# Causal attention with a mixture of experts: the order of value product and output projection within a step

## What is computed

```
x + attention(xn) + ffn(xn)

attention: q = (xn @ Wq + bq).reshape(b, h, t, dh)      16 heads of 128
           k, v = xn @ Wk + bk, xn @ Wv + bv            by head
           softmax(q k^T / sqrt(128), causal) @ v, heads joined, @ Wo + bo
ffn:       a shared expert, plus the best 6 of 64 experts per token,
           each expert with room for 128 tokens
```

## Time and profile before

| | |
|---|---|
| median of 3 runs (lowest, highest) | 2060.81 us (2058.49, 2063.56) |
| the profiled execution, its time | 2065.55 us |
| the profiled execution, its span | 2063.8 us |
| TensorE busy (matmuls) | 1683.7 us, 82% |
| VectorE busy | 1502.6 us, 73% |
| ScalarE busy | 1090.3 us, 53% |
| GpSimd busy | 1101.2 us, 53% |
| granted TensorE clock, mean over the span | 0.925 |

### The profile page before, as it was taken

The page is one execution under the profiler, slowest core; times in us unless marked ns, Lnnn a source line. Parts: engine busy times, 40 slices in busy tenths (PEclk is TensorE's granted clock), DMA queues, the critical chain, the costliest instruction groups (busy, mean ns, idle before and its releaser), DMA issues. The chain is left out here.

```text
span 2063.8 us, 49196 instructions
## 1 busy us (share of the span) xinstructions
PE 1683.7 (82%) x19016; PEld 1307.4 (63%) x19016; DVE 1502.6 (73%) x3148; ACT 1090.3 (53%) x2300; POOL 1101.2 (53%) x920
## 2 busy tenths in 40 slices
PE   1253089999999999999967788899899999888887
PEld 1242067777777777777756666677666666666665
DVE  5598956666667676666634478888888888888875
ACT  1520056666666666666622265555555555555564
POOL 0510046666666666666620066666666666666543
PEclk9676589999999999999977599999999999999999
DMA  5225067777665666656657566667666676667655
GB/s 182 102 102 196 0 129 135 134 136 129 123 110 104 123 103 101 105 103 104 109 130 218 171 112 121 119 120 147 120 122 121 117 139 120 122 119 144 118 90 109
DMA packets 695996, 253.35 MB, mean 123 GB/s; under 512 B 642384, under 2 KB 682145, under 8 KB 695008
## 3 DMA queue, kind: packets, MB, share of 16 engines
q1 hardware_dynamic: 668096, 204.12, 52.7%
q0 software_dynamic: 19232, 37.84, 7.2%
q10 hardware_dynamic: 8448, 8.39, 1.2%
HBM read 61.30 MB, written 54.66 MB: 56 GB/s over the span
## 5 line engine op out<-in xcount | busy, mean ns | idle before, releaser
L448 POOL TENSOR_TENSOR prob<-prob 128x128 f16<-128x128 f32 (+7 forms) x512 | 673.5, 1316 | 809.0 <-ACT prob L784 805.7
L777 ACT ACTIVATE prob<-prob,nmax 128x128 f32<-128x128 f32 (+7 forms) x512 | 398.0, 777 | 625.4 <-DVE prob L1135 568.0
L601 PE MATMUL ps_s<-kT,qT 128*128 128x512 f16 (+3 forms) x2304 | 460.6, 328 | 9.2 <-DVE prob L1135 5.7
L616 PE MATMUL ps_o<-probT,vh 128*128 128x256 f16 (+1 forms) x3840 | 434.4, 267 | 4.9 <-DMA probT<-prob 4.9
L1135 DVE TENSOR_SCALAR_CACHE_REDUCE prob<-ps_s,neg_scale 128x128 f32<-128x128 f32 (+7 forms) x512 | 408.8, 808 | 2.0 <-PE ps_s L603 1.8
L616 PEld LDWEIGHTS ps_o<-probT,vh 128*128 128x128 f16 x3840 | 372.0, 100 | 52.7 <-issue 5.8
L784 ACT CAST prob<-prob 128x128 f16<-128x128 f32 (+7 forms) x512 | 341.3, 667 | 2.9 <-DMA probT<-prob 0.6
L627 PE MATMUL ps_y<-wo,oT 128*128 128x256 f16 x1536 | 212.3, 275 | 126.5 <-DVE oT L1150 115.8
L601 PEld LDWEIGHTS ps_s<-kT,qT 128*128 128x128 f16 x2304 | 201.7, 99 | 162.9 <-issue 19.6
L567 PE MATMUL ps_t<-xT,wq 128*128 128x64 f16 x6144 | 195.2, 194 | 62.4 <-DMA xT<-xn_columns 61.0
L627 PEld LDWEIGHTS ps_y<-wo,oT 128*128 128x128 f16 x1536 | 136.2, 98 | 165.3 <-DVE oT L1150 136.7
(11 more groups left out here) (182 smaller groups left out, 1713.5 us busy)
## 6 DMA issues: line engine op xcount, KB each, us to landing
dispatched<-zeros SPq DMA_DIRECT2D x16, 512.0 KB, 5.4
probT<-prob SPq DMA_TRANSPOSE x512
ex<-dispatched SPq DMA_DIRECT2D x16, 512.0 KB, 4.3
expert_out<-eo ACTq DMA_DIRECT2D x16, 512.0 KB, 3.8
resid<-in_L_attn_x_dram SPq DMA_DIRECT2D x2, 2048.0 KB, 11.2
xn_rows<-xn SPq DMA_DIRECT2D x8, 512.0 KB, 3.0
xn_columns<-xnth SPq DMA_DIRECT2D x16, 256.0 KB, 2.3
xT<-xn_columns SPq DMA_DIRECT2D x8, 512.0 KB, 5.8
```

Of the source, the lines that this page charges most:

```text
L448: pool.tensor_tensor(low_cols(j), prob_cols(j).rearrange("p (r k) -> p r k", k=P), high_cols(j), ALU.subtract).then_inc(p_low, 1)
L601: pe.matmul(s_cols(j, lo, hi), qT[:, u, a, j * P:(j + 1) * P], kT[:, u, c, lo:hi], start=(n == 0), stop=(n == 2 and hi < w))
L616: mm = pe.matmul(ps_o[:, lo:2 * P], vh[:, u, a, r * D:(r + 1) * D], probT[:, PT_AT[c] + 2 * r + s, lo:], start=(r + n == 0), stop=(r == 2 ...
L777: nc.scalar.activation(prob_cols(j), prob_cols(j), ACT.Exp, bias=nmax[:, j:j + 1], scale=-1.0, accum_out=rsum[:, i % 2, j:j + 1]).then_inc ...
```

## The change

Three hand-written orders change; no instruction is added, removed or altered.

```diff
 TensorE, attention()
                     scores(i, 0)
+                    scores(i, 1)
                     if old:
+                        values(i - 1, 1)
                         project_y(i - 1, 0)
-                        values(i - 1, 1)
-                    scores(i, 1)
                     project_v(i, 0)
...
                     if old:
+                        values(i - 1, 2)
                         project_y(i - 1, 1)
-                        values(i - 1, 2)
...
                     if old:
+                        values(i - 1, 3)
                         project_y(i - 1, 2)
-                        values(i - 1, 3)
...
                     scores(i, 6)
+                    values(i, 0)
                     if old:
                         project_y(i - 1, 3)
-                    values(i, 0)
                     scores(i, 7)

 ScalarE, attention()
                     softmax_exp(i, 0)
+                    high_probs(i, 0)
+                    softmax_exp(i, 1)
                     if old:
                         high_o(i - 1, 1)
-                    high_probs(i, 0)
-                    softmax_exp(i, 1)
                     high_v(i, 0)

 VectorE, attention()
                     mix_at(1)
+                    block_max(i, 1)
                     if old:
                         scale_of_y(i - 1)
+                        low_o(i - 1, 1)
                         add_y(i - 1, 0, mixed(1))
-                        low_o(i - 1, 1)
-                    block_max(i, 1)
                     low_v(i, 0)
...
                     mix_at(5)
                     if old:
+                        low_o(i - 1, 3)
                         add_y(i - 1, 2, mixed(5))
-                        low_o(i - 1, 3)
...
                     mix_at(7)
+                    low_o(i, 0)
                     if old:
                         add_y(i - 1, 3, mixed(7))
-                    low_o(i, 0)
                     block_max(i, 7)
```

## The result

The changed kernel takes **2188.51 us** (median of 4 runs, 2187.25 to 2189.95); the kernel before, 2059.74 us on the same count. The ratio is 1.0622, with a 95% interval of 1.0604 to 1.0640: slower by 129 us. The forecast was 2191 us, 130 us more than before. Runs of the kernel before differ by up to 5 us within this comparison and by 8 us within a later one (2054.3 to 2062.5), so 2 us of agreement in the total prove nothing; the stretches of the step have to agree one by one.

A forecast was written before the change was run, and what follows sets the result against it. The VectorE and ScalarE chain was taken as the bound. First half +97 us and second half +33 give +130 us, some 2196 on the profiled 2065.55, lowered to 2191 us for the median; own range 2160 to 2215, whole range 2112 to 2240.

The forecast's parts named there:

- Slot 3, `low_o` before `add_y`: VectorE before block 5: `add_y(2)` now stands between `low_o(3)` and `low_q`, +0.73 us a step (first half), +0.79 (second).
- the port: Shared SBUF access: GpSimd's `low_probs(4)` gets in between the two `low_q`, so `block_max(5)` starts 1.21 us later a step.
- Rival (a): VectorE keeps the SBUF port for both `low_q`: 73 us less than forecast, 2118 us; chance 0.13.
- Slot 4: VectorE before block 7: `add_y(3)` now between `low_o(0)` and `block_max(7)`, +0.79 us a step (first half), +0.50 (second).
- Slot 1, first half: Blocks 0 to 2: `yscale` arrives behind GpSimd's 1024-column instruction and is blocked, `low_v` +0.45 us later a step.
- The handover of 0.1 us: Slot 1: estimated gap on VectorE between the end of the blocked `yscale` and `low_o(1)`, about 0.1 us.
- the 1.7 that I gave as a sign: Sign to look for: `yscale` averages about 1.7 us in the first half.
- Slot 1, second half: `block_max(1)` and the exponential pass the already blocked `yscale`: -1.62 us in 28 steps, +0.45 in 3, together -44 us.
- TensorE: Slot 2: next scores and q's projection start 1.0 us later, block 4's scores still ready 0.25 us early; nothing priced.
- Rival (b): TensorE becomes the bound: up to 1.6 us a step, halfway 48 us more, 2239 us; chance 0.15.
- Rival (c): Faster: value products first bring `high_o(3)` and `high_o(0)` 0.66 us earlier, slot 1's -45 us decides, 2016 us; chance 0.05.

The follow-up runs named there:

- e1: The changed kernel with VectorE's `add_y(2)` moved behind both `low_q`, still ahead of `block_max(5)`: 2115.1 us.
- e7: The kernel before, with `yscale` computed by `tensor_scalar` from one SBUF tensor and a scalar column: 2058.74 us.
- e6: The kernel before with the new orders of VectorE and ScalarE and TensorE's old one: 2254.66 us.
- e11: Against the kernel before: TensorE's new order, ScalarE's old; on VectorE `yscale` first in slot 1, `block_max(1)` next, later `add_y` behind `block_max` 4, 5, 7: 1982.63 us.
- e2: The changed kernel with VectorE's `add_y(2)` placed between the two `low_q`: 2157.85 us.
- e4: The changed kernel, with `yscale` computed by `tensor_scalar` from one SBUF tensor and a scalar column: 2188.64 us.
- e8: The kernel before, with the mixing operation of position 1 moved from ahead of `yscale` to behind `block_max(1)`: 2002.54 us.

## Why the prediction was right

By its own steps, measured by the two tables:

- **Slot 3, `low_o` before `add_y`, and the port.** Forecast +0.73 and +1.21 us in the first half, measured +1.98 together; in the second +0.79 and +1.21, measured +1.99. Over both halves that is 120 us forecast and 119 measured. e1 parts them: 1.21 us is the port. That GpSimd, arriving during a first VectorE instruction, gets the port before the second was read from `mix` and `yscale`; the 1284 ns in the mean over the 58 `low_q` of the first half's group (682 in e1) say that it holds throughout. Rival (a), 73 us less, is what e1 gives when the collision is taken away, not what the port does.
- **Slot 4.** Forecast +0.79 and +0.50, measured +0.78 and +0.50.
- **Slot 1, first half.** Forecast +0.45, measured +0.25 (7.09 to 7.34 us from block 0 to 2). The handover of 0.1 us that I estimated behind `yscale` does not exist: `low_o(1)` starts at 598.66, 0.07 us before `yscale` ends by the records, and `add_y` takes no more than before. That part was mis-sized, 6 us in all. `yscale` itself is held for 2.00 us, not the 1.7 that I gave as a sign: `block_max(1)` delays it by 0.23 us and not by 0.5. That cost nothing, since it ends with GpSimd either way.
- **Slot 1, second half.** Forecast -44 us in all, measured -46 (9.75 to 8.14 us from block 0 to 2, by the medians). ScalarE's exponential 1, which waited 3.20 us in a step before, no longer waits in the step of the changed kernel that I looked at.
- **TensorE.** I had q's projection start 1.0 us later, but checked only whether block 4's scores would still be ready. Between `block_max(3)` and `block_max(4)` stands `full_q`, which needs q's projection, and that already came late before in part of the steps (18 waits from 290 to 1030 us, 4.4 us in all; 27 and 9.5 us in the changed kernel, rows below the list). Block 3 to 4 costs 5.6 us in the first half and 1.7 in the second. So a term that I took at zero, without a look at `full_q`, is 7 us; that it offsets slot 1's is luck, and the 2 us of agreement in the total is luck as well. Part of it may be no effect of the change: e7, which has the orders of before, takes 2.42 us in 3 to 4 and 4.42 in 4 to 5 of the first half, instead of 2.75 and 4.20.
- **The range of the forecast's own terms.** By the terms as given its lower end is 2191 - 60 x 0.21 - 31 x 0.75 = 2155 us, not 2160. Nothing hangs on it.
- **Rival (b), TensorE as the bound.** Not seen beyond these 7 us: 2 to 4 in the second half, where (b) saw up to 1.6 us a step, is 5.60 us before and after, and the mean clock is 0.930 after and 0.925 before. In e6 and e11 TensorE does limit a stretch.
- **Rival (c)** would have needed `high_o(3)` earlier behind the exponential. It starts 0.51 us behind `high_q(0)`, the 0.06 us earlier that the forecast allowed, and no more.

The waits of VectorE for q's projection, before and then changed, 290 to 1030 us:

```profile
DVE qf L1110 <- PE ps_t L567: 4.4, 18, 0.4
```
```profile
DVE qf L1110 <- PE ps_t L567: 9.5, 27, 0.5
```

The rule of the Trainium skill (SBUF — State Buffer, Who interferes with whom), that the second to issue is fully blocked, agrees with the 2003 ns of `yscale` and with e2. That VectorE loses the port to a waiting GpSimd between two instructions this section of the skill does not say; the rows do. It also names two SBUF inputs or a two-port mode as the condition; e4's one-tensor multiplication is held as well, which the first condition does not cover. Whether it ran in a two-port mode no run here shows.

## What to carry to other kernels

On an engine that works in order, ask of every instruction whether it stands in a wait or behind one: the same 0.8 us of `add_y` cost nothing ahead of `low_o` and the full price behind it. Then look at what a shift of some tenths of a microsecond makes collide: here 73 of the 129 us lost and most of the 57 us gained by e8 came from whether an SBUF-only VectorE instruction starts just before or just after a long GpSimd one. An order on one engine is good or bad only together with the order of the engine that it waits for.

## What was not expected of the hardware

An 8-element multiplication with a single SBUF tensor input and a scalar column waits for GpSimd exactly as one with two tensors does (2007 ns in the mean, 0.23 us alone). And VectorE instructions issued back to back do not keep the port: GpSimd got in between the two `low_q` in the step shown, and the timelines of the other steps show the same: 2.48 us for the two, or 1.89 for the second where it stands alone, in all 60.
